# Group 0's attention operands written straight from matmuls, TensorE given early work, and later projections planned later

## What is computed

```python
# layer 1: attention a (16 heads; a head's q and k are 8 own columns and 32 "r" columns that q and k share)
q = (x @ Wq + bq).reshape(B, S, 16, 8);  k = (x @ Wk + bk).reshape(B, S, 16, 8);  v = (x @ Wv + bv)...
r = (x @ Wr + br).reshape(B, S, 16, 32)
q = concatenate([q, r], -1);  k = concatenate([k, r], -1)
attn = softmax(einsum('bqhd,bkhd->bhqk', q / sqrt(40), k));  out = einsum('bhqk,bkhd->bqhd', attn, v) @ Wo + bo
# then a mixture of 8 experts (top 1), layer 2: attention b (two softmaxes a head, rotated q and k), the experts again
x = x + attention_a(layernorm(x)); x = x + ffn(layernorm(x)); x = x + attention_b(layernorm(x)); x = x + ffn(layernorm(x))
```

## Time and profile before

| | |
|---|---|
| median of three runs (lowest to highest) | 1563.1 us (1561.01 to 1567.91) |
| the profiled execution: its own time | 1556.33 us |
| the profiled execution: span | 1554.6 us |
| busy PE, DVE, ACT, POOL | 1391.3, 1179.0, 1078.2, 693.7 us |
| share of PE, DVE, ACT, POOL in the chain that ended last | 63%, 12%, 7%, 7% |
| share of DMA landings and of SP's queue in it | 2%, 3% |

### The profile page before, as it was taken

One profiled execution on the slowest core, in us unless ns is written; L12 is line 12 of the kernel. 1 busy time (PEld: TensorE's weight loads), 2 busy tenths in 40 slices (PEclk: granted clock), 3 DMA queues, 4 the chain that ended last, 5 costly groups with the idle time before them and its releaser, 6 DMA issues.

```text
span 1554.6 us, 27029 instructions
## 1 busy us (share of the span) xinstructions
PE 1391.3 (89%) x9196; PEld 595.0 (38%) x9196; DVE 1179.0 (76%) x2024; ACT 1078.2 (69%) x1833; POOL 693.7 (45%) x758
## 2 busy tenths in 40 slices
PE   4999999999999999889998899998898999998656
PEld 1323334335554333445442323223233544442246
DVE  5767788877778688676788898997998777878233
ACT  1556666666566667777777788886888888877512
POOL 3312333324413744488866343423245875541023
PEclk8999999999999999899999999998999999998869
DMA  6577576855762324645412562202126534300034
GB/s 116 149 243 221 173 237 196 258 176 147 235 195 68 88 70 150 202 141 172 130 45 68 177 193 83 69 22 62 42 62 222 176 111 131 110 23 29 1 114 153
DMA packets 130286, 204.53 MB, mean 132 GB/s; under 512 B 16851, under 2 KB 96368, under 8 KB 130150
## 3 DMA queue, kind: packets, MB, share of 16 engines
q1 hardware_dynamic: 120558, 188.96, 41.0%
q0 software_dynamic: 6016, 12.71, 2.4%
q10 hardware_dynamic: 3576, 1.15, 0.5%
HBM read 123.40 MB, written 76.84 MB: 129 GB/s over the span
## 4 chain that ended last, share of the span: by engine, by line
PE 63%; DVE 12%; ACT 7%; POOL 7%; issue 5%; SPq 3%; DMA 2%; ACTq 0%; DVEq 0%; POOLq 0%
PE ps L1186 18%; PE ps L1152 10%; PE ps L1173 10%; DVE Mb L1493 8%; PE ps L1282 6%; PE ps L1267 5%; ACT P L1369 5%; PE ps L1120 4%; POOL ROW L1437 3%; PE ps L1194 3%; POOL rs L1715 1%; PE ps L1220 1%; DVE X L1652 1%; PE ps L1239 1%; SPq L908 1%
## 5 line engine op out<-in xcount | busy, mean ns | idle before, releaser
L1493 DVE TENSOR_REDUCE Mb<-ps 128x1 f32<-128x512 f32 (+1 forms) x970 | 931.7, 996 | 198.4 <-PE ps L1152 193.0
L1369 ACT ACTIVATE P<-ps 128x512 f32<-128x512 f32 (+1 forms) x1123 | 799.8, 759 | 204.3 <-PE ps L1173 171.3
L1173 PE MATMUL ps<-STK 32*128 32x512 f16 (+1 forms) x1536 | 420.3, 389 | 29.1 <-ACT P L1369 18.2
L1152 PE MATMUL ps<-STK 32*128 32x512 f16 (+1 forms) x1536 | 408.7, 389 | 38.1 <-DVE Mb L1493 11.2
L1186 PE MATMUL ps<-P,V 128*32 128x512 f32 x3072 | 418.1, 617 | 9.4 <-ACT P L1369 8.3
L1152 PEld LDWEIGHTS ps<-STK 32*128 32x128 f16 (+1 forms) x1536 | 103.8, 94 | 284.4 <-DVE Mb L1493 95.5
L1173 PEld LDWEIGHTS ps<-STK 32*128 32x128 f16 (+1 forms) x1536 | 108.0, 93 | 268.3 <-ACT P L1369 87.8
L1764 POOL DMA_INDIRECT xs<-ROW,slot x64 | 63.6, 994 | 151.4 <-DVE slot L1583 136.4
L1186 PEld LDWEIGHTS ps<-P,V 128*32 128x32 f32 x3072 | 60.9, 108 | 126.9 <-issue 102.3
L1267 PE MATMUL ps<-XT,WE 128*128 128x128 f32 x696 | 96.9, 283 | 4.8 <-issue 2.1
L1267 PEld LDWEIGHTS ps<-XT,WE 128*128 128x128 f32 x696 | 86.1, 193 | 22.2 <-issue 8.2
(11 more groups left out here) (156 smaller groups left out, 1365.9 us busy)
## 6 DMA issues: line engine op xcount, KB each, us to landing
WE<-wx SPq DMA_DIRECT2D x87, 576.0 KB, 4.3
STK<-qka SPq DMA_DIRECT2D x56, 480.0 KB
qka<-HL SPq DMA_DIRECT2D x84, 256.0 KB, 4.0
STK<-qkb SPq DMA_DIRECT2D x64, 256.0 KB
xs<-pad SPq DMA_DIRECT2D x8, 1554.0 KB, 8.2
qkb<-HL SPq DMA_DIRECT2D x96, 128.0 KB, 2.4
X<-xs SPq DMA_DIRECT2D x73, 129.5 KB, 3.0
qka<-HL SPq DMA_DIRECT2D x42, 128.0 KB
```

The lines of the kernel that those rows point to most:

```text
L1152: mm = eng.matmul(ps[:, bank + i, :], l_, r_, start=True, stop=True)
L1173: mm = eng.matmul(ps[:, bank + i, :], l_, r_, start=True, stop=True)
L1369: eng.activation(P[:, st % 3, j:j + n, :], ps[:, bank:bank + n, :], ACT.Exp, scale=SCALE_A if g < 4 * B else SCALE_B).then_inc(sem("exp"), 1)
L1493: eng.tensor_reduce(Mb[:, g % 2, at:at + 4 * n - 3:4], ps[:, bank:bank + n, :], AX, ALU.max).then_inc(sem("mx"), 1)
```

## The change

Five edits.

1. **Group 0's operands by matmuls.** The host lays out a weight tile `lw` of 8 x 120 columns: for head j and side w the columns of r three times and of q or k three times. Eight matmuls (`lead`) give 120 partitions each, already in the place in which STK wants them. ACT (`lead_hi`, with a scale of 0 or 1 a partition) writes 0 where a hi part is wanted and the hi part where a lo part is wanted, and DVE (`lead_lo`) subtracts that and writes STK itself. The 12 copies of group 0 go; `feat` has five tiles in batch 0 instead of six, and its parts are split by POOL as in the other batches. `lw` (480 KB) is the first load on ACT's queue.
2. **All of `direct` on SP's queue**, 36 DMAs; those of the groups 2 and 3 wait until the maxima of group 0 have been written (`mr0`).
3. **16 matmuls of ones at the start** (128x512, bfloat16) into the bank of `pv`, before the first transpose.
4. **Batches 1 and 2 held back**: in the plan, four of batch 1's projections wait for exponentials of group 0, and batch 2's transpose for the scores of group 1.
5. Costs of `columns` in the plan, and the waits' values that follow from edit 1.

```diff
-MOST = {"score": 3, "smax": 4, "other": 3}
+MOST = {"lead": 6, "score": 3, "smax": 4, "other": 3}
...
     def direct(g, w):
-        yield from after(("flo", (w,)), ("flo", (2 + g,)))
-        yield from do(g - 8 + w / 2, "direct", g, w, **(dict(engine="scalar", us=2.8) if (g, w) == (0, 1) else {}))
+        yield from after(*[("split", (n,)) for n in (1, 2, 2 + g)])
+        if g > 1:
+            yield from after(("mput", (0,)))
+        yield from do(g - 8 + w / 2, "direct", g, w)
...
             if b == 1:
                 yield from after(("maxima", (0,)))
+            if b == 2:
+                yield from after(("scored", (1,)))
...
     def features(b, n, rank):
+        if b == 1 and n > NA + 1:
+            yield from after(("exped", (0, n - NA - 2)))
...
             def direct(g, w):
-                direct_on(eng, on, g, w)
+
+                on.wait_ge("split", 2 + g)
+                if g > 1:
+                    on.wait_ge("mr0", 16)
+                for o in range(3):
+                    i = 1 if o == 2 - w else 0
+                    eng.dma_start(SA[96 + 8 * o:104 + 8 * o, g, w], HL[32 * g:32 * g + 32, 1 + w, i, :]).then_inc(sem(f"tp{g}"), 16)
+                    eng.dma_start(SA[32 * o:32 * o + 32, g, w], HL[:, 2 + g, i, :]).then_inc(sem(f"tp{g}"), 16)
...
+            def lead(i):
+
+                bank = bank_for("lead", i)
+                on.wait_ge("ld_wa", 112)
+                on.wait_ge("htc", 1)
+                eng.matmul(ps[0:120, bank, :], LW[:, 120 * i:120 * i + 120], HT[:, 0, :], start=True, stop=True).then_inc(sem("lp"), 1)
...
+                if g == 0:
+                    on.wait_ge("ll", 2 * (c % 4 + len(ring["smax", (g, c)])))
+                elif c == 0:
                     on.wait_ge(f"tp{sl}", tp_count(g))
...
+            on.wait_ge("cst", 6)
+            for i in range(16):
+                eng.matmul(ps[:, OB, :], ones[:, :], ones[:, :].rearrange("p (o n) -> p o n", o=1).broadcast_to([128, 4, 128]),
+                           start=True, stop=True)
...
+            def lead_hi(i):
+
+                on.wait_ge("lp", i + 1)
+                on.wait_ge("ld_wa", 112)
+                w = i % 2
+                eng.activation(LH[0:120, i // 2, 512 * w:512 * w + 512], ps[0:120, bank_of("lead", i)[0], :], ACT.Identity,
+                               bias=FB[0:120, NA + 8 + i:NA + 9 + i], scale=FB[0:120, NA + 16 + w:NA + 17 + w]).then_inc(sem("lh"), 1)
...
+            def lead_lo(i):
+                on.wait_ge("lh", i + 1)
+                w = i % 2
+                eng.scalar_tensor_tensor(out=SA[0:120, 0, w, i // 2, :], in0=ps[0:120, bank_of("lead", i)[0], :],
+                                         scalar=FB[0:120, NA + i:NA + 1 + i], in1=LH[0:120, i // 2, 512 * w:512 * w + 512], op0=ALU.add,
+                                         op1=ALU.subtract).then_inc(sem("ll"), 1)
...
+                if n < NA:
+                    pass
+                elif n < 2 * NA:
+                    for g in range(1, DIRECT):
                         on.wait_ge(f"tp{g}", DIRECTS)
```

More of the change, by code:

```diff
@@ L276, in row_maxima @@
             rank = g - 1.92
-            yield from after(*([("stack", (g,))] if g >= DIRECT else [("direct", (g, 0)), ("direct", (g, 1))]))
+            if g:
+                yield from after(*([("stack", (g,))] if g >= DIRECT else [("direct", (g, 0)), ("direct", (g, 1))]))
             if g >= 2:
@@ L281, in row_maxima @@
             while c < 16:
+                if g == 0:
+                    yield from after(("lead_lo", (2 * min(3, c % 4 + 1) + 1,)))
                 yield from fill_pair(rank + c / 16, "smax", g, c)
@@ L344, in direct, with leads, lead_parts @@
     def direct(g, w):
-        yield from after(("flo", (w,)), ("flo", (2 + g,)))
-        yield from do(g - 8 + w / 2, "direct", g, w, **(dict(engine="scalar", us=2.8) if (g, w) == (0, 1) else {}))
+        yield from after(*[("split", (n,)) for n in (1, 2, 2 + g)])
+        if g > 1:
+            yield from after(("mput", (0,)))
+        yield from do(g - 8 + w / 2, "direct", g, w)
+    def leads():
+        yield from after(("hcopy", (0,)))
+        for i in range(8):
+            yield from fill_bank(-2.3 + i / 50, "lead", i)
+            spawn(lead_parts(i))
+    def lead_parts(i):
+        yield from do(-2.3 + i / 50, "lead_hi", i)
+        yield from do(-2.3 + i / 50, "lead_lo", i)
+        give("lead", i)
     def outs():
@@ L420, in projections @@
             give("hturn", b)
-            for x in range(nt):
-                spawn(features(b, n0 + x, rank + 1.15 * span(b) * x / nt))
+            for x in range(0 if b else 1, nt):
+                spawn(features(b, n0 + x, rank + 1.15 * span(b) * x / nt if b else -1.6))
             spawn(values_of(b, last))
     def features(b, n, rank):
+        if b == 1 and n > NA + 1:
+            yield from after(("exped", (0, n - NA - 2)))
         yield from fill_bank(rank, "feat", n)
         if b < B:
+            if n >= 5:
+                yield from after(("split", (n - 4,)))
+            yield from do(rank, "fhi", n)
+            give("feat", n)
+            if b:
+                yield from after(*([("direct", (g, w)) for g in range(1, DIRECT) for w in range(2)] if b < 2 else [("put", (n - HLN,))]))
+            yield from do(rank, "split", n)
             if b < 1:
-                yield from do(rank, "fhi", n)
-                yield from do(rank, "flo", n)
-                give("feat", n)
                 return
[L433 to L439, removed]
             if b >= 3:
@@ L675, in wake @@
                 step(job, max([t] + [ended[e] for e in events]) if ask[0] == "after" else t)
-    for job in [setups(), scores(), exps(), values(), row_maxima(), reduces(), maxima_back(), norms(), outs(), stacks(), *[direct(g, w) for g in range(DIRECT) for w in range(2)], projections(), norm_in(), loads(), batch_ends(), second_weights(), mixed(), blanks(),
+    for job in [setups(), scores(), exps(), values(), row_maxima(), reduces(), maxima_back(), norms(), outs(), stacks(), *[direct(g, w) for g in range(1, DIRECT) for w in range(2)], leads(), projections(), norm_in(), loads(), batch_ends(), second_weights(), mixed(), blanks(),
                 fetch_weights(range(M0)), fetch_rows(range(M0)), fetch_weights(TAIL), fetch_rows(TAIL)] + [
@@ L737, in schedule @@
     return (order, ring, times) if ticks else (order, ring)
-FIRST = {"split": NA, "stack": DIRECT, "put": NA, "raw": NA * B, "xload": 4}
+FIRST = {"split": 1, "feat": 1, "fhi": 1, "stack": DIRECT, "put": NA, "raw": NA * B, "xload": 4}
 def build(nc, a):
@@ L878, in freed @@
                 "hturn": lambda: ("htc", i + 1),
-                "feat": lambda: ("flo", i + 1) if i < NA else ("fhi", i + 1) if i < NA * B else ("raw", i - NA * B + 1),
+                "lead": lambda: ("ll", i + 1),
+                "feat": lambda: ("fhi", i) if i < NA * B else ("raw", i - NA * B + 1),
                 "vproj": lambda: ("vb", v_count(i) - (1 if i >= B and index[1] == 0 else 0)),
@@ L1284, in down @@
                 mm.then_inc(sem("fo"), 1)
-            stages = dict(hturn=hturn, feat=feat, vproj=vproj, smax=smax, mrow=mrow, score=score,
+            on.wait_ge("cst", 6)
+            for i in range(16):
+                eng.matmul(ps[:, OB, :], ones[:, :], ones[:, :].rearrange("p (o n) -> p o n", o=1).broadcast_to([128, 4, 128]),
+                           start=True, stop=True)
+            stages = dict(lead=lead, hturn=hturn, feat=feat, vproj=vproj, smax=smax, mrow=mrow, score=score,
                           pv=pv, oturn=oturn, aturn=aturn, oproj=oproj, gturn=gturn, glogit=glogit, gplace=gplace, wsum=wsum, xturn=xturn, up=up,
```

99 lines of the change are left out of this document (50 added, 49 removed).

## The result

The changed kernel takes 1589.89 us (median of 5 runs, 1582.71 to 1591.53), the kernel before 1563.1. The ratio is 1.0123, 95% interval 1.0082 to 1.0164: 1.2% or 19 us slower (13 to 26). The bare medians stand further apart, 26.8 us or 1.7%; the text goes by the ratio. The forecast was +5.0 us, at most 1577. The profiled execution took 1582.71 us, with a span of 1580.9, 26.3 us longer than that of before.

What follows compares the result with a forecast made beforehand. The chain of copies, puts and DMAs up to `stack(4)` sets group 4's start, then PE. Copies +11.5, SP's order -6.4, the read -0.4 give +4.7; DVE's maxima 0.3: +5.0 on 1563.1, so 1568.1 us, range 1556 to 1577.

Steps and rivals of the forecast that it cites:

- The loads: At the start, `lw` ahead of bst on ACT's queue delays layer norm and the first lead: +2.0 us, bounds 0.5 and 3.3.
- The upper bound of 3.3 us: Delay of bst at the start if SP's queue shares the DMA engines half and half with ACT's; 1.3 us above the forecast.
- The warm-up and the leads: Before group 0: PE's clock likely lost before the leads, +2.0 us; group 0's maxima end at 39.5, `mr0` at 43.9.
- The copies and `stack(4)`: Last copy lands 11.5 us late, at 64.7; 6.4 and 0.4 us come back at `stack(4)`; group 4 starts at 92.3, +4.7.
- The pause: Ahead of group 4, PE would stand idle for some ten us, until 92.
- Holding batch 2's projections is free: its operands are needed at group 8, 40 us later: Between groups 4 and 8: delaying batch 2's projections was claimed to cost nothing.
- All else is reshuffled with equal work, which I hold to be worth nothing on the mean and 4 us either way: Rest of the program: the new order adds nothing on the mean, 4 us either way; DVE's extra maxima count 0.3 us.
- The signs of being wrong: Profile findings that would refute the forecast: no pause ahead of group 4, `stack(4)` before 85, or 5 us not staying until the end.
- the rest's order the larger term: Last refuting sign: the start comes as forecast, but its 5 us do not stay until the end; no size given.
- the slower rival: Cold leads +1.4, later bst +1.3, new order behind group 4 +3: +10.7 us in all, 1574 us; chance 0.24.
- its single mechanism: At the leads, PE stays at 1.2 GHz through all 13 projections: +8.9 us on top, 1577 us; within the slower side's 0.24.

Runs made afterwards that it cites:

- e1: The changed kernel without the hold on batch 2, which gives another order; ratio to the kernel before 1.0145.
- e10: The kernel before up to the start of group 1, then the changed kernel's order on every engine and SP's queue; ratio to the kernel before 1.0141.
- e3: The kernel before with only the plan's cost of `columns` set to the changed kernel's value, which alters the order alone; ratio 0.9993.
- e13: The changed kernel with `stack(8)` moved ahead of a put and two weight pieces on SP's queue; ratio to the kernel before 1.0106.
- e7: The changed kernel with the old cost of `columns` in the plan, which gives another order; ratio to the kernel before 1.0129.
- e14: The kernel before up to a point planned at 543 us, then the changed kernel's order; ratio to the kernel before 1.0048.
- e15: The changed kernel up to a point planned at 543 us, then the old order; ratio to the kernel before 1.0096.
- e16: The changed kernel planned and run without the `mr0` wait up to group 8, then the order of the kernel before; ratio to the kernel before 0.9944.
- e9: The changed kernel's start, with its `mr0` wait, then the order of the kernel before on every engine and SP's queue; ratio to the kernel before 1.0064.
- e11: The changed kernel with the same plan and order, only SP's wait for `mr0` removed; ratio to the kernel before 1.0112.
- e5: The kernel before with the tile of biases 18 unused columns wider, same instructions and order; ratio to the kernel before 0.9994.

## Why the prediction was wrong

**The loads, right.** bst lands at 2.22 + 5.16 = 7.38 (forecast 7.4), the first lead starts at 14.11 (14.1). The upper bound of 3.3 us would have put it 1.3 us later; the trace does not show that. The prediction had tied that bound to the Trainium skill's rule that engines take turns between queues ("DMA: Bandwidth & Descriptors", "Queues, rings and completion order"). How much SP's queue had to move meanwhile was not looked at, so the rule itself is neither borne out nor refuted here.

**The warm-up and the leads, right.** The clock was lost before the first lead, as forecast (granted 0.5 from 10.2 to 17.0 us): 2.03 + 1.37 us for two projections that take 0.86 each when warm, 1.7 us in all (forecast 2.0). The maxima's turn by PE is at 39.41 (their end forecast for 39.5), `mput` was issued at 40.14 (40.9), and SP went on at 43.69 (43.9).

**The copies and `stack(4)`, the mechanism right, the size 3.1 us too large.** The last copy was issued at 59.17 (59.7) but landed after 3.72 us, not 5.0: 62.9 (64.7). From there to `stack(4)`'s issue it took 19.3 us (18.8), and from that issue to group 4 7.0 us (8.9). So group 4 started at 89.2, +1.6 us for the forecast +4.7. I had taken both landings from rows of before with more in the queue; that this made them shorter is argued, not tested. The pause is there: PE is busy for 2.69 of the 10 us up to 90.

**"Holding batch 2's projections is free: its operands are needed at group 8, 40 us later": right of the hold, wrong of the place.** The hold costs nothing that e1 shows; what it gains at group 4 is gone at group 8. And I did not read the new queue at group 8, where `stack(8)` now stands behind batch 3's puts and two weight pieces, and PE waited 5.79 us.

**"All else is reshuffled with equal work, which I hold to be worth nothing on the mean and 4 us either way": this is the step that failed.** The order of the rest alone is worth +1.4% (e10, 16 to 28 us) with the old start, and takes up all of the 19 us that the changed kernel is slower by. The work is equal within 4.4 us of DVE, and from group 16 to 48 PE is busy for 509 us within 1 us either way, and the stretch is 4.3 (e10) and 7.8 us (the change) longer. The set from 48 to 64 is longer by 6.8 to 14.2 us in every run that has that order. I took the 4 us from nothing: no row of before stood behind it. The signs of being wrong named it last ("the rest's order the larger term"), and the slower rival sized it at 3 us (and its single mechanism, a PE that stays cold in the leads, didn't occur). The order was there to be compared ahead of the run; it would have shown `stack(8)` behind its new neighbours, and I know of nothing in it that would have shown the rest.

**What stays open.** Shown is that the order costs, how much, and in which stages. Which property of it does so is not. It isn't the number of paired maxima (e3), the wait at group 8 alone (e13, e7), or one place (e14, e15). In the set from 48 to 64 it goes with stretches at the lower clock: 3.4 to 24 us in all in each of the seven runs of the new order, none in four of the five of the old (10 us in e15). From 16 to 48 the change and e10 lose idle time of PE at an equal clock (0.98), with 7 to 8 us more of DVE's work; the six executions of the new order took 541.3 to 545.9 us there, three of the old one 532.8 to 538.0, but e16, also with the old one, 546.6. That short pauses bring the clock down is argued from e10's one place, not shown by an experiment.

The whole loss isn't the clock. The record has the mean granted clock of every execution: 0.963 in the profiled one of the change and 0.960 in that of before; 0.957 in e10's and 0.958 in e9's, which lie 16 us apart. On e10's chip the five executions of e10 have 0.959 on the mean and the 17 of before 0.965. Executions of the kernel before, 88 on four chips, differ among themselves by about 11.6 us for 0.01 of clock. By an estimate from that slope, some 7 of e10's 24 us (difference of the means) go with the clock, and 12 of e7's 19 (0.956 for 0.966); the rest doesn't.

## What to carry to other kernels

A planner that is fed new work at the start makes a new order for the whole program, and that order is an edit of its own: here +1.4%, more than all that was changed on purpose. Freeze the order behind the edited part (old list, new start) before you judge the edit. Here the change's start with the old order behind it (e9) lost 0.6% instead of 1.2%; with the wait for `mr0` dropped too, the planner's own order (e8) stood at -0.1%, not told from zero, and the frozen one (e16) at -0.6%. And look past the first wait: the start's visible gain of 6.5 us at group 0 was given back at group 4 because later copies waited for it, and dropping that wait made group 4 6.7 us earlier than before with the same order (e11), 9.9 with the order that the plan then makes (e8).

## What was not expected of the hardware

- **With one order a stage repeats to 0.1 us, with another it doesn't.** Groups 48 to 64 took 192.5, 192.5, 192.4 and 192.4 us in before, e5, e9 and e16, all with the old order and at a clock of 1.00 there, though they begin up to 14 us apart. With the new order, and PE's matmuls equal within four, seven executions took 199.3 to 206.7 us at a clock of 0.94 to 0.99. So the 6.8 us by which the shortest of these is longer is no noise, but the new order's own spread is as large.
- **PE stays at 1.2 GHz while it is busy.** In e10 the lower level held from 982 to 998 us with PE busy for 15.22 of 16 us. From the Trainium skill ("TensorE: Matmul & The Clock Gate", "Part 1: The HAM clock gate"), by which activity releases the throttle, one would have looked for the full clock sooner; the trace decides. (The same part also tells of a kernel whose clock fell and rose again with short idle times between groups of matmuls.) What it costs: the rows of groups 48 to 64 give e10 2 x (1 - 0.94) x 206.7 = 25 us at that level and the changed kernel 2 x (1 - 0.99) x 199.3 = 4, with the same order, and e10 takes 7.4 us longer, about 0.35 us for each.
- **Matmuls of ones ahead of a pause buy little.** PE worked from 2.06 to 8.01 us, paused for 4.22, and the first lead was as slow as in e4 without them; 0.9 of the 2.5 us that cold projections cost in e4 was saved.
